# Two dense tiles of the last expert layer computed ahead of its sorted blocks

## What is computed

```python
scores = einsum('bsd,td->bst', x, sign(tile_sigs))   # x = layernorm(h)
idx = argmax(scores, axis=-1)                        # one of T = 8
all_out = einsum('bsd,tde->bste', x, W) + b
out = take_along_axis(all_out, idx, axis=2)
h = h + out
```

## Time and profile before

| What | Value |
|---|---|
| Time, median of 3 runs | 1627.62 us |
| Lowest and highest of them | 1624.96 and 1629.68 us |
| The profiled execution's own time | 1619.05 us |
| Its span, first to last instruction | 1617.2 us |
| Its mean granted PE clock | 0.97 |
| Instructions | 22240 |

### The profile page before, as it was taken

How to read it: one execution, slowest core, us unless ns; L and a number is a source line. 1 busy time by engine, 2 the same in 40 slices (tenths; PEclk the granted TensorE clock), 3 DMA queues, 4 the chain that set the end, 5 groups by cost and what they waited for, 6 DMA issues and landing times.

```text
span 1617.2 us, 22240 instructions
## 1 busy us (share of the span) xinstructions
PE 1522.4 (94%) x7946; PEld 1102.0 (68%) x7946; DVE 784.4 (49%) x1691; ACT 503.6 (31%) x1002; POOL 441.1 (27%) x433
## 2 busy tenths in 40 slices
PE   6999989987999999999999999999989998998889
PEld 5543345467999999999996555678864445666763
DVE  3668989973111111111107774013675564887704
ACT  1366555521122122222214522222310005655330
POOL 1457878812111111111114000000010001332272
PEclk9999999998999999999999997999999999999899
DMA  6345444544167465412312002001000001000033
GB/s 192 107 107 151 130 109 128 117 163 169 73 213 250 139 217 192 152 52 79 128 52 72 1 1 75 0 0 53 1 1 1 0 0 53 1 1 20 20 105 114
DMA packets 54181, 139.10 MB, mean 86 GB/s; under 512 B 9356, under 2 KB 33061, under 8 KB 47397
## 3 DMA queue, kind: packets, MB, share of 16 engines
q1 hardware_dynamic: 47492, 121.79, 23.5%
q0 software_dynamic: 5760, 15.74, 3.1%
q10 hardware_dynamic: 816, 0.14, 0.0%
HBM read 202.24 MB, written 14.03 MB: 134 GB/s over the span
## 4 chain that ended last, share of the span: by engine, by line
PE 67%; DVE 12%; issue 1%; ACT 1%; DMA 1%; POOL 1%; DVEq 0%; SPq 0%; ACTq 0%; POOLq 0%
PE psum L823 41%; PE psum L1149 10%; PE psum L855 6%; DVE work L1917 2%; DVE work L2058 2%; PE psum L833 1%; DVE work L2057 1%; PE psum L920 1%; PE psum L1003 1%; DVE bst L1568 1%; PE psum L1189 1%; PE psum L1198 1%; DVE work L2066 1%; DVE sq L1596 1%; PE psum L858 1%
## 5 line engine op out<-in xcount | busy, mean ns | idle before, releaser
L823 PE MATMUL psum<-work 128*128 128x128 f32 (+3 forms) x3400 | 472.9, 301 | 9.3 <-DMA tokb<-in_tokb 9.3
L823 PEld LDWEIGHTS psum<-work 128*128 128x128 f32 x3400 | 442.6, 194 | 26.6 <-DMA tokb<-in_tokb 9.3
L1985 DVE TENSOR_TENSOR work<-sq,psum 128x512 f32<-128x512 f32 x82 | 56.3, 687 | 392.4 <-PE psum L823 392.4
L2111 POOL TENSOR_TENSOR rs<-rs,power 128x4 f32<-128x4 f32 (+3 forms) x40 | 44.6, 1116 | 476.2 <-DVE rs L1575 469.9
L2147 POOL TENSOR_TENSOR work<-work,w_late 128x408 f32<-128x408 f32 (+1 forms) x160 | 160.3, 1051 | 38.2 <-DVE work L1917 24.2
L1917 DVE TENSOR_TENSOR_SCAN work<-psum,work 128x414 f32<-128x414 f32 (+1 forms) x160 | 156.8, 1052 | 7.6 <-ACT psum L1361 7.2
L1149 PE MATMUL psum<-w_late,xn 128*128 128x512 f32 x352 | 155.6, 600 | 0.6 <-ACT work L1253 0.6
L920 PE MATMUL psum<-work,xn 128*128 128x408 f32 (+1 forms) x320 | 141.8, 564 | 11.7 <-DVE work L1935 6.5
L2173 POOL DMA_INDIRECT y_rows<-sq,row_of x41 | 40.5, 987 | 363.6 <-ACT sq L1253 363.6
L1361 ACT ACTIVATE psum<-work,a_neg 128x408 f32<-128x408 f32 (+1 forms) x160 | 100.0, 627 | 81.3 <-DVE work L1917 81.3
L1794 DVE SCALAR_TENSOR_TENSOR h<-psum,gate,h 128x256 f32<-128x256 f32 x176 | 76.9, 479 | 99.7 <-PE psum L1149 95.8
(11 more groups left out here) (286 smaller groups left out, 2064.5 us busy)
## 6 DMA issues: line engine op xcount, KB each, us to landing
work<-in_W SPq DMA_DIRECT2D x123, 1024.0 KB
w_attn<-in_unit SPq DMA_DIRECT2D x96, 192.0 KB, 3.0
w_late<-c_rows SPq DMA_DIRECT2D x48, 204.0 KB, 3.2
w_late<-c_rows SPq DMA_DIRECT2D x32, 238.0 KB, 3.7
work<-y_rows SPq DMA_DIRECT2D x11, 512.0 KB, 6.0
work<-in_unit SPq DMA_DIRECT2D x22, 192.0 KB, 5.1
w_late<-in_we SPq DMA_DIRECT2D x2, 2048.0 KB, 8.2
work<-in_xp SPq DMA_DIRECT2D x1, 2700.0 KB, 15.4
```

Source lines behind the costliest of these rows:

```text
L823: mm = pe.matmul(dst, lhs(k), rhs(k), start=(k == 0), stop=(k == parts - 1))
L1985: dve.tensor_tensor(hm[:, j % 2, 4 * q:4 * q + 4, :].rearrange("p k n -> p (k n)"), sa[:, i % 2], A.at(("e3", j, q)), ALU.mult).then_inc(s ...
```

## The change

`plan_dx` is split off from `plan_dense`: it allots the eight banks of a duo's dense products and puts the duo's `dense` step into PE's list. For layer 2 of the two dense layers (r = 2, the last layer), duo 6's is called ahead of xT3(0); `plan_dense(2, ...)` then begins with `gateT` and the bias of duo 6 and goes on with duos 7 and 8 as before. For r = 1 nothing changes. Only PE's order and the order of bank allotments differ; the other engines' programs keep their order.

```diff
+        def plan_dx(r, d):
+            for q in range(QUADS):
+                for i in DUO_TILES[d]:
+                    bank_of[r, i, q] = len(bank_of) + 1
+                    W8.plan(("dx", r, i, q), (sem("summed"), sums_to(r, d, q) + i - DUO_TILES[d][0] + 1))
+            step("dense", r, d)
+
         def plan_dense(r, block):
             for d in range(DENSE_D0[r], DUOS):
-                for q in range(QUADS):
-                    for i in DUO_TILES[d]:
-                        bank_of[r, i, q] = len(bank_of) + 1
-                        W8.plan(("dx", r, i, q), (sem("summed"), sums_to(r, d, q) + i - DUO_TILES[d][0] + 1))
-                step("dense", r, d)
+                if d > DENSE_D0[r] or r == 1:
+                    plan_dx(r, d)
                 if d == DENSE_D0[r]:
                     plan_gateT(r)
                 W8.plan(("db", r, d), (h_ready, H(block + 1, d)))
...
             step("xT3", j)
 
+        plan_dx(2, SORT_D)
         for j in range(XT3 - 1):
             plan_xT3(j)
```

## The result

The change measured 1619.81 us against 1627.51 us for the kernel before, both the median of 12 runs (1612.37 to 1622.41, and 1620.37 to 1631.76). The medians differ by 7.7 us. The ratio of the runs is 0.9948, with a 95% interval of 0.9933 to 0.9964, which is 8.5 us less (between 5.9 and 10.9). The forecast was 1621.0 and faster, and both came true. The profile shows that the number came out better than its working.

What follows compares the result with a forecast made beforehand. PE's list was taken to set the end. Moved products 13.97, new wait 1.35, refill 0.2, blocks 28.8 and copy wait 0.55 make 44.9 us against 51.5, a gain of 6.6: 1627.6 to 1621.0 us, range 1617.0 to 1625.5.

Steps and rivals of the forecast that it cites:

- The bound and the place: PE's list sets the end; products moved behind the logits take 13.97 us at full clock, with eight banks free.
- The new wait: Before xT3(0), whose bank is freed by VectorE's sixteenth sum, PE and the queued blocks stand still for 1.35 us.
- The refill: At the first block, ey3(0) needs ACT's copy of xT3(0); two more transpose pairs cover most of it, leaving 0.2 us.
- The clock: PE's granted clock does not fall behind the new 1.35 us wait before xT3(0); priced at no loss.
- the clock rival: PE's clock falls behind the new wait or is low when moved products begin; gain 3.2 to 4.9 us; chance 0.20.
- Gathers, scatters, sorted tail: On POOL and SP, gathers 11 to 18 and all scatters slip 4.4 us; no block starves; tail hidden, slack 7 us.
- The total: Whole kernel: 6.6 us gained, 1627.6 to 1621.0 us, 0.4% less.

Runs made afterwards that it cites:

- dead-work run: Kernel before plus 16 recorded products with unread results between the router logits and xT3(0), nothing moved; ratio to before 0.9995 (0.9977 to 1.0012).
- rotated ring: The change with the banks of xT3 and ey3 in the order 3, 4, 5, 0, 1, 2; ratios to the kernel before 0.9942 and 0.9952.
- third profile: The changed kernel profiled and timed once more without any edit; its timing gave a ratio to the kernel before of 0.9977 (0.9960 to 0.9993).
- clock kept: The change plus twelve transposes that nobody reads between the moved products and xT3(0); ratio to the kernel before 0.9963 (0.9945 to 0.9980).
- duo 6 whole: The change with duo 6's gate transposes and bias also put ahead of the blocks; 1607.01 us against 1616.22 for the kernel before, ratio 0.9946.
- two quads: The change with only quads 0 and 1 of duo 6 ahead of the blocks, the others behind; ratio to the kernel before 0.9951 (0.9929 to 0.9973).

## Why the prediction was right, and where it was wrong

*The bound and the place: right.* PE's list sets the end before and after; the products moved fit behind the logits at full clock (13.9 us) with all eight banks free, and the dead-work run shows that the time they went into was empty.

*The new wait: right in kind, size 1.45 us for 1.35.* It was found by counting the ring; the rotated ring removes it. VectorE's last sum ends at 1549.34 in the third profile and PE starts at 1549.48, so the hand-off took 0.14 us and not 0.04.

*The refill: mis-sized, 0.61 to 0.63 us for 0.2.* Three transpose pairs are there, but PE waits for ACT all the same: ACT's three copies end at 0.94 us together. Without the wait ahead of it the same refill costs only 0.23 us (both profiles of the rotated ring, and the dead work). With the wait filled by transposes it is 0.64, so it is not the idle time as such that makes it long. The cause stays open.

*The clock: the step that failed.* "I price it at no loss" rested on one wait of 1.34 us behind which the clock held in one profile. Behind that same wait it fell for 3.4 us in seven of thirteen. Here, behind 1.45 and 0.61 us with 0.85 us of transposes between, it fell in three profiles of three, for 3.4 us, costing 1.7. I had this as a rival at 0.20 with a gain of 4.9 us; it is what happened to the stretch. Whether it falls here always, and whether the two idle pieces count together, is not shown: no run had the first piece without the second. The second alone, 0.64 us in clock kept and 0.79 in duo 6 whole, brought no fall. The Trainium skill (TensorE: Matmul & The Clock Gate, Part 1) says that slow stretches vary from run to run with the monitor's phase. The traces agree for the wait of 1.34 us (seven falls in thirteen profiles) and for the gate transposes (two in the four profiles with both waits); behind the new wait three profiles are too few to tell. By seven in thirteen the rival's chance was nearer one half than 0.20.

With these three the sum is 44.9 + 0.1 + 0.4 + 1.7 = 47.1 us, against 47.2 and 47.3 measured. The stretch thus gains 4.5 us (5.2 by G, of which up to 1 us can be the early logits), and not 6.6.

*Gathers, scatters, sorted tail: right.* The twelfth gather slipped from 13.9 us behind the first to 17.7 (3.8 us; 4.4 forecast), no block waited for rows, SP had its last stores ahead of VectorE.

*The total: right in part by luck.* The stretch did what the clock rival says, and by that the time should have been 1622.7 or a little more; it came out at 1619.8, near a forecast whose working was 2.2 us too good. The three timings of the change give 8.5, 4.8 and 3.7 us, 5.7 in the mean. The 5.2 us of G lies within the second and third interval, and 0.7 us outside the first (5.9 to 10.9). Part of the first may be scatter of the other layers: before the first gather, where the programs are identical, the eleven profiles of the experiments reached it between 1524.0 and 1534.2 us. The three profiles of the kernel before are all late there (1534.7, 1534.0, 1534.1), those of the change earlier (1531.9, 1529.7, 1532.6), but the rotated ring stood once at 1524.0 and once at 1533.8. Whether something in it belongs to the kernels stays open; the runs here can't tell.

## What to carry to other kernels

Where an engine that sets the end idles for data that are being fetched, put independent work there, as long as the idle time and no more: two quads gave what four gave with the rotated ring. When work is moved in an allocation ring, count which buffer the steps behind it inherit. Here it was the very last one to be freed, and shifting the ring by one gained nearly as much again as the change itself (4.4 us beside some 4.5, 0.7 of them from a second inherited bank). Price a wait on TensorE from the same wait in several profiles: the one of 1.34 us lowered the clock in seven of thirteen and cost nothing more in the rest. Filling the wait, with useful work or even with dead work, kept the clock in the runs here.

## What was not expected of the hardware

- One wait of 1.34 us behind 10 us of solid matmul work lowered the clock for 3.4 us in seven profiles and left it at 1.00 in six; the programs are the same up to there.
- A wait of 1.45 us plus 0.61 us lowered it for 3.4 us in three profiles of three; with dead transposes in the same place (one profile) it held.
- ACT stopped once for 5.24 us, in one of thirteen profiles, while inputs for it piled up. PE's wait for it (4.16 us) and the low clock behind it (6.8 us, 3.4 lost) made S 7.4 us longer (54.7 against 47.3). Its cause was not found.
- Seven microseconds of added matmuls left the time the same (0.9995, interval 0.9977 to 1.0012).
